# Chunked inputs of the clipped scan, and later stores of parts with interleaved maxima in three 16-head attentions

## The chip, the cores and the metric

The kernel runs on one core of one Trainium2 chip, as one program. The metric is the device time of one execution in microseconds (us); a result is the median of several executions. Engines: PE is TensorE (PEld its weight loads), DVE is VectorE, ACT is ScalarE, POOL is GpSimd, SP is SyncE. "ACTq" and "SPq" are the sequencers of ACT and SP issuing DMAs.

## The reference

A network of four layers works on X of 2048 tokens by 128. Each layer adds to X, in turn, a mixer, a feed-forward part and an attention (or the same in another order), twelve sublayers in all. The change touches four of them. Three are attentions of 16 heads of size 8:

```python
q, k, v = (heads(Wq, bq), heads(Wk, bk), heads(Wv, bv))
cos, sin = _rope_cos_sin(T, D)
q = _apply_rope(q, cos, sin)
k = _apply_rope(k, cos, sin)
att = jnp.einsum('bhqd,bhkd->bhqk', q, k) * (1.0 / np.sqrt(D))
att = jnp.where(causal[None, None], att, NEG_BIG)
att = jax.nn.softmax(att, axis=-1)
y = jnp.einsum('bhqk,bhkd->bhqd', att, v)
```

That is L0b, causal and rotary. L2b is the same without rotation and mask, and L3b has q and k filtered over the tokens instead; these two are called plain here. The fourth sublayer, L1a, is a scan with clipped states:

```python
xc = jax.lax.conv_general_dilated(xc, conv_w, window_strides=(1,), padding=[(K - 1, 0)], ...)
xi = _silu(jnp.transpose(xc, (0, 2, 1)))
dt_low = jnp.einsum('bld,rd->blr', xi, x_proj_w)
delta = jax.nn.softplus(jnp.einsum('blr,dr->bld', dt_low, dt_proj_w) + dt_proj_b)
delta = jnp.clip(delta, 1e-06, 10.0)
A = jnp.clip(-jnp.exp(A_log), -10.0, -1e-06)
e = jnp.clip(jnp.exp(delta * A), 1e-06, 1.0)
```

after which state = clip(state * e + xi) runs over the tokens. Here 256 channels are two halves of 128, and K is 4 taps.

## The kernel before, in words

The program is a sequence of stages. Each stage is one or a few blocks, and all engines meet at a block's end: none starts the next block before the slowest has issued its last instruction of this one. X, its normed copy nT and other activations lie in SBUF as [128, 2048] in fp32; a chunk is 512 tokens (CW), NC = 4 chunks.

**Attention, preparation** (`prepare_heads`). q and k are each split into three bf16 parts (high, middle, low), made by DVE (L777) and ACT (L791); DVE doubles two of the q parts (L781). A head's scores come from one matmul with 123 rows: products of parts, stacked, and rows that subtract the maxima. For that the parts of head 0 are copied by SP (L717, L722) straight into the row tiles qs[0], ks[0]; for all other heads the parts are stored by ACT's queue in DRAM (`store_part`, `store_twice`: eight DMAs of 512 KB, L725, L726, L729), from where SP loads each head's rows. ACT issues the stores last, after its copies of v (L794).

**Attention, heads** (`head_loop`). For each head the maxima of the scores per query are computed first: a "unit" is one tile of 128 queries by up to 1024 keys, two matmuls with 48 rows (L994) into one of two PSUM tiles (mps), in the causal case with the mask added by another matmul (L1000) on the diagonal, then one reduction by DVE (L1133). There are U = 24 units a head when causal, 32 when plain. When a head's units are reduced, DVE joins them (L1119), POOL splits them into three bf16 parts (L427 to L431), PE turns them (L1008, `turn_max`), ACT copies them (L1086), and a DMA puts them into row 72 and following of qs (L1096 by ACT for head 0, L946 by SP for the others). Only then can the head's scores start (L1018, S = 40 tiles when causal, 64 when plain), three PSUM tiles (SB), each with an exponential on ACT (L1105), then the products with v (L1039, L1042) into `ops`, which ACT copies out once a head (L1092) at its exponential n = OUT of the next head.

PE's stream is fixed: before head 0's scores it issues U + 3 units, `turn_max(0)` and 5 units more (U + AHEAD). After that, behind score n of head h, it issues units until `due(h, n)` are done, so that the next head's units run under this head's scores, two at a time (BURST). `turn_max(h + 1)` stands after score TURN = S - 7. In the causal case a pair of units signals DVE together (`ins.then_inc(mx_ready, len(xs))`). DVE joins head h - 1 after its first reduction of head h. SP in `head_loop` waits for the stores, then loads the rows of head 1, the missing half of head 0, the small products, and two heads ahead from there on.

In the trace these are stages 5, 8 and 9 (L0b: rows, preparation, heads), 36, 38, 39 (L2b) and 59, 63, 64 (L3b).

**Scan, inputs and decays** (`causal_scan_layer`, stages 13 to 18). After the input projection five blocks follow: the taps on DVE over all 2048 tokens (L1292, L1294) with silu on ACT (L1301); two projections (L361, 8 matmuls each) with copies by ACT and DVE; `softplus` (L1356 to L1368) with Exp and Ln in turn on ACT; and the decays (L1312 to L1329). Then `clipped_scan` begins (L1393).

## Time and profile before

| | |
|---|---|
| median of 3 runs | 5204.46 us (5199.28, 5204.46, 5205.0) |
| profiled execution | 5199.7 us, span 5197.9 us |
| busy: PE, DVE, ACT, POOL | 86%, 62%, 51%, 19% |
| mean granted clock of PE | 0.918 |
| causal attention's heads | from 364.3 us to about 910 us |
| plain attentions' heads | from 2461.5 us and from 4183.8 us |
| scan's inputs and decays | 1228.2 to 1292.3 us |

The granted clock is the share of 2.4 GHz that TensorE got, so 0.50 is 1.2 GHz. A row of the timeline gives the start, the busy time of a run of like instructions, the engine, the line, the operation, and in brackets how long the engine idled before and what released it.

### The profile page before, as it was taken

The page shows a single profiled execution, that of the slowest core. Times are in us where ns is not written, and L with a number is a line of the kernel's source. Part 1 is how long each engine was busy: PE and PEld are TensorE (multiplying, and loading weights), DVE is VectorE, ACT ScalarE, POOL GpSimd, SP SyncE. Part 2 cuts the span into 40 slices and gives each one's busy share as a digit, 9 for nine tenths or more (in the row PEclk, how much of TensorE's full clock was granted, in tenths as well). Part 3 has the DMA queues.
Part 4 walks back from the last instruction along what each step waited for, and adds up shares of the span by engine and source line. Part 5 has one row for each costly group of instructions (what it writes and reads, how often), then busy time and mean ns, then how long its engine had stood idle before and what let it go on. Part 6 is the DMA issues. An engine that isn't in the chain of part 4 may idle for free. (4 is left out here: it accounts for less than half of the span.)

```text
span 5197.9 us, 65865 instructions
## 1 busy us (share of the span) xinstructions
PE 4488.1 (86%) x22389; PEld 1663.4 (32%) x22441; DVE 3223.0 (62%) x4634; ACT 2648.4 (51%) x4913; POOL 976.2 (19%) x920
## 2 busy tenths in 40 slices
PE   6978888795189999867999997688869889999899
PEld 3432222442033333243122223355544412222244
DVE  4366664435865555254988883437963488888433
ACT  2325666334224444433588885344433348888633
POOL 0000000000038777800000000047940000000000
PEclk8979999897599999978899998898979979999999
DMA  1011110000000000001100000110000010000000
GB/s 62 20 67 35 35 35 20 17 16 0 7 1 3 5 3 5 5 28 37 36 28 28 27 18 2 56 62 3 1 9 16 11 68 26 26 26 26 3 21 20
DMA packets 44620, 118.99 MB, mean 23 GB/s; under 512 B 14463, under 2 KB 15863, under 8 KB 43287
## 3 DMA queue, kind: packets, MB, share of 16 engines
q1 hardware_dynamic: 37235, 98.19, 5.7%
q10 hardware_dynamic: 4524, 15.78, 0.8%
q8 instruction: 166, 2.72, 0.2%
q0 software_dynamic: 2560, 1.19, 0.1%
q14 instruction: 135, 1.11, 0.1%
HBM read 87.89 MB, written 19.01 MB: 21 GB/s over the span
## 5 line engine op out<-in xcount | busy, mean ns | idle before, releaser
L1133 DVE TENSOR_REDUCE 64_heads_mx<-64_heads_mps 128x1 f32<-128x1024 f32 x512 | 604.1, 1220 | 64.3 <-PE 64_heads_mps L994 63.1
L1133 DVE TENSOR_REDUCE 39_heads_mx<-39_heads_mps 128x1 f32<-128x1024 f32 x512 | 604.1, 1220 | 64.3 <-PE 39_heads_mps L994 63.2
L1105 ACT ACTIVATE 64_heads_p<-64_heads_sps 128x512 f32<-128x512 f32 x1024 | 552.8, 596 | 111.2 <-PE 64_heads_sps L1018 107.3
L1105 ACT ACTIVATE 39_heads_p<-39_heads_sps 128x512 f32<-128x512 f32 x1024 | 552.7, 596 | 111.3 <-PE 39_heads_sps L1018 107.3
L2106 ACT ACTIVATE 27_latent_heads_p<-27_latent_heads_ring 128x512 f32<-128x512 f32 x512 | 277.3, 595 | 385.4 <-PE 27_latent_heads_ring L2025 374.1
L1133 DVE TENSOR_REDUCE 9_heads_mx<-9_heads_mps 128x1 f32<-128x1024 f32 (+7 forms) x384 | 334.2, 908 | 179.7 <-PE 9_heads_mps L1000 173.3
L2124 DVE TENSOR_REDUCE 27_latent_heads_mx<-27_latent_heads_ring 128x1 f32<-128x512 f32 x512 | 323.1, 684 | 197.4 <-PE 27_latent_heads_ring L2005 197.4
L1105 ACT ACTIVATE 9_heads_p<-9_heads_sps 128x512 f32<-128x512 f32 (+3 forms) x640 | 304.3, 535 | 190.0 <-PE 9_heads_sps L1021 161.6
L1018 PE MATMUL 64_heads_sps<-59_head_rows_qs,59_head_rows_ks 123*128 123x512 bf16 x1024 | 311.3, 386 | 4.9 <-ACT 64_heads_p L1105 4.9
L1018 PE MATMUL 39_heads_sps<-36_head_rows_qs,36_head_rows_ks 123*128 123x512 bf16 x1024 | 310.9, 385 | 5.2 <-ACT 39_heads_p L1105 5.2
L1981 POOL TENSOR_TENSOR 27_latent_heads_psum<-27_latent_heads_psum,27_latent_heads_p 128x1024 f32<-128x1024 f32 x112 | 263.1, 2349 | 87.8 <-ACT 27_latent_heads_p L2106 87.8
L2021 PE MATMUL 27_latent_heads_ring<-27_latent_heads_qc,23_mla_mem_keys 64*128 64x512 f32 x1024 | 272.7, 609 | 3.4 <-DMA 24_mla_loop_mem_mrow<-27_latent_heads_mT 3.4
L1042 PE MATMUL 39_heads_ops<-39_heads_p,L2b_v 128*9 128x512 f32 x2048 | 267.8, 595 | 0.2 <-ACT 39_heads_osb L1092 0.2
L1042 PE MATMUL 64_heads_ops<-64_heads_p,L3b_v 128*9 128x512 f32 x2048 | 267.8, 595 | 0.2 <-ACT 64_heads_osb L1092 0.2
L1976 POOL TENSOR_TENSOR 27_latent_heads_psum<-27_latent_heads_psum,27_latent_heads_p 128x1024 f32<-128x1024 f32 x112 | 263.3, 2351 | 23.0 <-ACT 27_latent_heads_p L2106 23.0
L2005 PE MATMUL 27_latent_heads_ring<-23_mla_mem_keys,27_latent_heads_qc 64*128 64x512 f32 x1024 | 265.1, 609 | 1.9 <-DVE 27_latent_heads_mx L2124 0.5
L994 PE MATMUL 64_heads_mps<-59_head_rows_ks,59_head_rows_qs 48*128 48x512 bf16 x1024 | 187.6, 403 | 23.3 <-PEq L755 15.3
L994 PE MATMUL 39_heads_mps<-36_head_rows_ks,36_head_rows_qs 48*128 48x512 bf16 x1024 | 187.7, 403 | 18.1 <-PEq L755 10.0
L1018 PE MATMUL 9_heads_sps<-5_head_rows_qs,5_head_rows_ks 123*128 123x512 bf16 (+3 forms) x640 | 183.4, 353 | 11.5 <-ACT 9_heads_p L1105 4.3
L427 POOL CAST 64_heads_mparts<-64_heads_m 128x16 bf16<-128x16 f32 x16 | 3.1, 196 | 973.9 <-DVE 64_heads_m L1119 973.9
L615 DVE TENSOR_TENSOR 4_experts_hg<-4_experts_hr,4_experts_gps 128x512 f32<-128x512 f32 x128 | 88.0, 687 | 147.8 <-ACT 4_experts_hr L602 147.5
L615 DVE TENSOR_TENSOR 67_experts_hg<-67_experts_hr,67_experts_gps 128x512 f32<-128x512 f32 x128 | 88.0, 688 | 146.4 <-ACT 67_experts_hr L602 146.1
(1119 smaller groups left out, 7456.7 us busy)
## 6 DMA issues: line engine op xcount, KB each, us to landing
44_hale_masks_qs<-scratch_q_parts SPq DMA_DIRECT2D x45, 96.0 KB
44_hale_masks_ks<-scratch_k_parts SPq DMA_DIRECT2D x45, 96.0 KB
4_experts_wbuf<-in_L0f_experts SPq DMA_DIRECT2D x8, 514.0 KB, 3.5
12_experts_wbuf<-in_L0f_experts SPq DMA_DIRECT2D x8, 514.0 KB, 3.4
58_experts_wbuf<-in_L3f_experts SPq DMA_DIRECT2D x8, 514.0 KB, 3.5
67_experts_wbuf<-in_L3f_experts SPq DMA_DIRECT2D x8, 514.0 KB, 3.5
5_head_rows_qs<-scratch_q_parts SPq DMA_DIRECT2D x47, 64.0 KB
5_head_rows_ks<-scratch_k_parts SPq DMA_DIRECT2D x47, 64.0 KB
```

The costliest lines, as they stand in the source:

```text
L615: dve.tensor_tensor(hg[n % SLOTS][:], hr[n % SLOTS][:], gps[n // NF % 2][:], ALU.mult).then_inc(hg_ready, 1)
L994: ins = pe.matmul(mps[x % 2][:, b:b + n], qs[h % SETS][low:low + SIX, tile(i)], ks[h % SETS][low:low + SIX, 1024 * half + b:1024 * half + ...
L1018: ins = pe.matmul(sps[e % SB][:, 0:CW - off], ks[h % SETS][0:SUM_ROWS, tile(j)], qs[h % SETS][0:SUM_ROWS, c * CW + off:(c + 1) * CW], star ...
L1042: ins = pe.matmul(ops[row:row + ROW, off:CW], Vt[:, j, h, :], p, start=(s == 0), stop=(causal or s == NG - 1), tile_position=(0, row), ski ...
L1105: act.activation(pslot[x % PS][:, 0:CW - off], sps[e % SB][:, 0:CW - off], ACT.Exp, scale=SCALE / 2).then_inc(ex_done, 1)
L1133: dve.tensor_reduce(mx[h % 2][:, i, half:half + 1], mps[x % 2][:, 0:w], AX.X, ALU.max).then_inc(mx_taken, 1)
L1976: pool.tensor_tensor(psum[:, 0, :], so_far, slot(p, h)[:], ALU.add).then_inc(added_even, 1)
L1981: pool.tensor_tensor(psum[:, 1, :], so_far, slot(p, h)[:], ALU.add).then_inc(added_odd, 1)
L2005: pe.matmul(bank(number, x)[:], qc[h % 2][half, tile(i)], keys[half, chunk(2 * (u % 2) + x)], start=True, stop=True).then_inc(mx_ready, 1)
L2021: pe.matmul(bank(number, x)[:], keys[half, tile(j)], qc[h % 2][half, chunk(2 * (p % 2) + x)], start=True, stop=False)
L2106: act.activation(slot(p, h)[:, x * CW:(x + 1) * CW], bank(score_number(p, h), x)[:], ACT.Exp, scale=MLA_SCALE).then_inc(ex_done, 1)
L2124: dve.tensor_reduce(mx[:, w // NC, w % NC:w % NC + 1], bank(max_number(w // 2, h), w % 2)[:], AX.X, ALU.max).then_inc(mx_taken, 1)
```

## The change

1. `HeadRows.store` gathers the eight stores. In the three attentions (those with `doubled`) ACT issues them no longer at the end of `prepare_heads` but at the start of its stream in `head_loop`, once head 0's copies have landed. A fourth user of `prepare_heads`, a local attention, keeps them in place.
2. SP loads the rows of head 1 behind head 0's second half and small products.
3. `FIRST` and `WAIT` replace part of AHEAD for head 0: causal, 24 units and `turn_max(0)` stand before the scores, and the units of head 1 are issued behind scores 8 to 27; plain, 34 units, `turn_max(0)`, 2 units. DVE joins head 0 before its first reduction of head 1.
4. Each unit signals DVE by itself, a diagonal one after its own mask.
5. OUT is 4 in the causal case.
6. The scan's inputs and decays become one block, `causal_inputs`, by chunks: the first tap on ACT, three on DVE, silu, both projections and their copies chunk by chunk; then all eight Exp, all eight Ln, all eight decays.

```diff
                 eng.dma_start(self.ks[0][DH * i:DH * (i + 1), :], self.k[a][0:DH, :]).then_inc(self.rows_in[0], 16)

-    def store_part(self, g, eng, a):
-        eng.dma_start(g.scratch["q_parts"][a], self.q[a][:]).then_inc(self.stored, 16)
-        eng.dma_start(g.scratch["k_parts"][a], self.k[a][:]).then_inc(self.stored, 16)
-
-    def store_twice(self, g, eng, n):
-        eng.dma_start(g.scratch["q_parts"][3 + n], self.twice[n][:]).then_inc(self.stored, 16)
+    def store(self, g, eng):
+        for a in range(3):
+            eng.dma_start(g.scratch["q_parts"][a], self.q[a][:]).then_inc(self.stored, 16)
+            eng.dma_start(g.scratch["k_parts"][a], self.k[a][:]).then_inc(self.stored, 16)
+        for a, t in enumerate(self.twice):
+            eng.dma_start(g.scratch["q_parts"][3 + a], t[:]).then_inc(self.stored, 16)

...
                                    ACT.Identity).then_inc(v_done, 1)
-                for a in range(3):
+                if not doubled:
                     for s in "qk":
-                        wait_for_part(act, s, a)
-                    rows.store_part(g, act, a)
-                for n in range(len(twice)):
-                    act.wait_ge(two_done, n + 1)
-                    rows.store_twice(g, act, n)
+                        for a in range(3):
+                            wait_for_part(act, s, a)
+                    rows.store(g, act)
...
+    FIRST, WAIT = (0, 8) if causal else (4, 0)
     TURN = S - 7
     LATE = 4 if causal else 6
     BURST = 2
-    OUT = 6
+    OUT = 4 if causal else 6
     A = P // HEADS
     N = HEADS * S
     qs, ks, rows_in = rows.qs, rows.ks, rows.rows_in
...
         def due(h, n):
-            return min(HEADS * U, U + AHEAD + h * U + (n + 1) * U // (S * BURST) * BURST)
+            steady = min(HEADS * U, U + AHEAD + h * U + (n + 1) * U // (S * BURST) * BURST)
+            if h:
+                return steady
+            begun = max(0, n + 1 - WAIT)
+            return min(steady, U + FIRST + begun * (U - FIRST) // ((TURN - 5 - WAIT) * BURST) * BURST)

...
-        assert U + AHEAD + (TURN - 4) * U // S >= 2 * U
+        assert due(0, TURN) >= 2 * U
...
                 sp.wait_ge(rows.filled, rows.FILLED)
                 sp.wait_ge(rows.stored, rows.STORED)
-                load_rows(sp, 1)
                 for a in range(3):
                     load_queries(g, sp, 0, a, qs[0], m_in[0], (1,))
                     load_keys(g, sp, 0, a, ks[0], m_in[0], (1,))
                 load_products(sp, 0)
+                load_rows(sp, 1)
                 load_products(sp, 1)
                 sp.dma_start(spread[:], g.big["head_spread"].rearrange("p (a q) -> p a q", q=P)).then_inc(spread_in, 16)
...
+                        if not diag:
+                            ins.then_inc(mx_ready, 1)
                     for x in xs:
                         _i, _half, w, diag = units[x % U]
                         if diag:
-                            ins = pe.matmul(mps[x % 2][:, w - P:w], g.ident_bf[:], g.mask_q[:], start=False, stop=True)
-                    ins.then_inc(mx_ready, len(xs))
+                            pe.matmul(mps[x % 2][:, w - P:w], g.ident_bf[:], g.mask_q[:], start=False, stop=True).then_inc(mx_ready, 1)

                 def turn_max(h):
                     e = turned(h)
...
-                while x < U + 3:
+                while x < U + FIRST // 2:
                     max_pass([x])
                     x += 1
                 turn_max(0)
-                while x < U + AHEAD:
+                while x < U + FIRST:
                     max_pass([x])
                     x += 1
                 late = []
...
+                act.wait_ge(rows_in[0], SIX_COPIED)
+                rows.store(g, act)
                 copy_max(0)
                 act.wait_ge(ex_done, 1)
                 act.dma_start(qs[0][TWICE:SUM_ROWS, :], mT[0][:]).then_inc(m_in[0], 16)
...
+                    if u == 0 and h == 1:
+                        join_max(0)
                     dve.wait_ge(mx_ready, x + 1)
                     dve.tensor_reduce(mx[h % 2][:, i, half:half + 1], mps[x % 2][:, 0:w], AX.X, ALU.max).then_inc(mx_taken, 1)
-                    if u == 0 and h:
+                    if u == 0 and h >= 2:
                         join_max(h - 1)
                 join_max(HEADS - 1)
                 for i in range(2):
...
-            dt_low = inner.sb("dt_low", [64, T])
...
-            project(g, "dt_low", [Job(dt_low, [(W["L1a_xproj"][:, 0:64], u[0]), (W["L1a_xproj"][:, 64:128], u[1])])], ready)
-            project(g, "dt", [Job(acc[i], [(W["L1a_dtproj"][:, i * P:(i + 1) * P], dt_low)], W["L1a_dtb"][:, i:i + 1])
-                              for i in range(2)], ready)
-            softplus(g, acc, xi)
...
+            causal_inputs(g, xi, acc, u, e)
         states = [g.nT, g.yT]
...
+def causal_inputs(g, xi, acc, u, e):
...
+        low_ps = [st.ps(f"low{i}", [P, CW]) for i in range(2)]
+        dt_ps = [st.ps(f"dt{i}", [P, CW]) for i in range(6)]
...
+                low_rank(0)
+                for c in range(1, NC):
+                    low_rank(c)
+                    step_sizes(c - 1)
+                step_sizes(NC - 1)
...
+                act.wait_ge(padded, 2)
+                tap(0)
+                tap(1)
+                silu(0)
+                copy_low(0)
+                tap(2)
+                silu(1)
+                copy_low(1)
+                copy_sizes(0)
+                tap(3)
+                silu(2)
+                copy_low(2)
+                copy_sizes(1)
+                silu(3)
+                copy_low(3)
+                copy_sizes(2)
+                copy_sizes(3)
+                act.activation(A[:], W["L1a_Alog"], ACT.Exp).then_inc(A_exp, 1)
+                for n, (c, i) in enumerate(steps):
+                    act.wait_ge(size_ready, n + 1)
+                    act.activation(xi[i][:, chunk(c)], xi[i][:, chunk(c)], ACT.Exp, scale=-1.0).then_inc(tail_exp, 1)
+                for n, (c, i) in enumerate(steps):
+                    act.wait_ge(tail_exp, n + 1)
+                    act.activation(xi[i][:, chunk(c)], xi[i][:, chunk(c)], ACT.Ln, bias=1.0).then_inc(tail_ln, 1)
+                act.wait_ge(A_done, 2)
+                for n, (c, i) in enumerate(steps):
+                    act.wait_ge(bounded, n + 1)
+                    act.activation(flat[i][:, chunk(c)], acc[i][:, chunk(c)], ACT.Exp, scale=A[:, i:i + 1]).then_inc(decayed, 1)
+
+                def other_taps(c):
+                    for k in range(1, K):
+                        for i in range(2):
+                            if k == 1:
+                                dve.wait_ge(first_tap, 2 * c + i + 1)
+                            else:
+                                dve.wait_ge(taps, 2 * (K - 1) * c + 2 * (k - 2) + i + 1)
+                            dve.scalar_tensor_tensor(acc[i][:, chunk(c)], xi[i][:, c * CW + k:(c + 1) * CW + k],
+                                                     W["L1a_conv"][:, i * K + k:i * K + k + 1], acc[i][:, chunk(c)],
+                                                     ALU.mult, ALU.add).then_inc(taps, 1)
...
+                other_taps(0)
+                other_taps(1)
+                other_taps(2)
+                other_taps(3)
+                for c in range(NC):
+                    size(c)
...
+                for n, (c, i) in enumerate(steps):
+                    dve.wait_ge(tail_ln, n + 1)
+                    dve.scalar_tensor_tensor(acc[i][:, chunk(c)], acc[i][:, chunk(c)], 0.0, xi[i][:, chunk(c)], ALU.max, ALU.add).then_inc(summed, 1)
+                    if n:
+                        bound(n - 1)
+                bound(NS - 1)
+                for n, (c, i) in enumerate(steps):
+                    dve.wait_ge(decayed, n + 1)
+                    dve.tensor_scalar(flat[i][:, chunk(c)], flat[i][:, chunk(c)], 1e-6, 1.0, ALU.max, ALU.min).then_inc(e_done, 1)
```

ACT's stream at the end of the preparation in L0b (9_heads_mT is head 0's maxima), the change as a difference:

```order
-L725 DMA scratch_q_parts<-5_head_rows_q 128x2048
-L726 DMA scratch_k_parts<-5_head_rows_k 128x2048
-L725 DMA scratch_q_parts<-5_head_rows_q 128x2048
-L726 DMA scratch_k_parts<-5_head_rows_k 128x2048
-L725 DMA scratch_q_parts<-5_head_rows_q 128x2048
-L726 DMA scratch_k_parts<-5_head_rows_k 128x2048
+L755 UNCONDITIONAL_BRANCH
+L1085 UNCONDITIONAL_BRANCH
+L726 DMA scratch_q_parts<-5_head_rows_q 128x2048
+L727 DMA scratch_k_parts<-5_head_rows_k 128x2048
```

The block ends at the branches. The stores stood ahead of them and now stand behind.

PE's stream in L0b around the turn of head 0's maxima (L1008, now L1014), before:

```order
L994 MATMUL 9_heads_mps<-5_head_rows_ks,5_head_rows_qs 128x512 x2
L1008 MATMUL 9_heads_sps<-ident_bf,9_heads_mparts 48x128
L994 MATMUL 9_heads_mps<-5_head_rows_ks,5_head_rows_qs 128x128
L1000 MATMUL 9_heads_mps<-mask_q_bf,ident_bf 128x128
L994 MATMUL 9_heads_mps<-5_head_rows_ks,5_head_rows_qs 128x512 x2
L994 MATMUL 9_heads_mps<-5_head_rows_ks,5_head_rows_qs 128x256
L1000 MATMUL 9_heads_mps<-mask_q_bf,ident_bf 128x128
L994 MATMUL 9_heads_mps<-5_head_rows_ks,5_head_rows_qs 128x512 x2
L994 MATMUL 9_heads_mps<-5_head_rows_ks,5_head_rows_qs 128x256
L1000 MATMUL 9_heads_mps<-mask_q_bf,ident_bf 128x128
L1018 MATMUL 9_heads_sps<-5_head_rows_qs,5_head_rows_ks 128x512
```

and after:

```order
L1014 MATMUL 9_heads_sps<-ident_bf,9_heads_mparts 48x128
L1024 MATMUL 9_heads_sps<-5_head_rows_qs,5_head_rows_ks 128x512
L1027 MATMUL 9_heads_sps<-mask_k_bf,ident_bf 128x128
L1024 MATMUL 9_heads_sps<-5_head_rows_qs,5_head_rows_ks 128x512 x3
L1024 MATMUL 9_heads_sps<-5_head_rows_qs,5_head_rows_ks 128x384
L1027 MATMUL 9_heads_sps<-mask_k_bf,ident_bf 128x128
L1024 MATMUL 9_heads_sps<-5_head_rows_qs,5_head_rows_ks 128x512 x3
L1045 MATMUL 9_heads_ops<-9_heads_p,9_heads_Vz 25x512 x4
```

No unit stands between the turn and the first scores any more.

The same place in L2b (stage 39, now 37; two L994, now L999, are one unit), before:

```order
L994 MATMUL 39_heads_mps<-36_head_rows_ks,36_head_rows_qs 128x512 x70
L1008 MATMUL 39_heads_sps<-ident_bf,39_heads_mparts 48x128
L994 MATMUL 39_heads_mps<-36_head_rows_ks,36_head_rows_qs 128x512 x10
L1018 MATMUL 39_heads_sps<-36_head_rows_qs,36_head_rows_ks 128x512 x4
L994 MATMUL 39_heads_mps<-36_head_rows_ks,36_head_rows_qs 128x512 x4
```

and after:

```order
L999 MATMUL 37_heads_mps<-34_head_rows_ks,34_head_rows_qs 128x512 x68
L1014 MATMUL 37_heads_sps<-ident_bf,37_heads_mparts 48x128
L999 MATMUL 37_heads_mps<-34_head_rows_ks,34_head_rows_qs 128x512 x4
L1024 MATMUL 37_heads_sps<-34_head_rows_qs,34_head_rows_ks 128x512 x4
L999 MATMUL 37_heads_mps<-34_head_rows_ks,34_head_rows_qs 128x512 x4
```

Forty units ahead of the first score become 36. Further on, in head 0, the 65th and 66th unit stand behind score 52 before and behind score 56 now, while the turn of head 1's maxima stands behind score 58 in both.

## Rows read from the trace of the kernel before

**Rows 1.** Timeline, causal attention, where the preparation ends and the heads start.

```profile
357.49 0.62 ACT L794 ACTIVATE L0b_v<-8_prepare_vps 128x512 f32<-128x512 f32 x1
...
361.46 2.39 ACTq L729 DMA_DIRECT2D scratch_q_parts<-5_head_rows_twice  x2
...
364.32 1.12 PE L994 MATMUL 9_heads_mps<-5_head_rows_ks,5_head_rows_qs 48*128 48x512 bf16 x3 [8.31 <-PEq L755]
```

**Rows 2.** Timeline, the same place in the first plain attention.

```profile
2455.26 0.61 ACT L794 ACTIVATE L2b_v<-38_prepare_vps 128x512 f32<-128x512 f32 x1
...
2461.51 1.44 PE L994 MATMUL 39_heads_mps<-36_head_rows_ks,36_head_rows_qs 48*128 48x512 bf16 x3 [9.97 <-PEq L755]
```

**Rows 3.** Timeline, causal attention, from head 0's last maxima to its first scores.

```profile
393.64 1.22 DVE L1133 TENSOR_REDUCE 9_heads_mx<-9_heads_mps 128x1 f32<-128x1024 f32 x1
...
394.77 0.17 DVE L1119 TENSOR_REDUCE 9_heads_m<-9_heads_mx 128x16 f32<-128x32 f32 x1
...
397.02 1.38 ACTq L1096 DMA_DIRECT2D 5_head_rows_qs<-9_heads_mT  x1
...
404.07 0.61 PE L1018 MATMUL 9_heads_sps<-5_head_rows_qs,5_head_rows_ks 123*128 123x512 bf16 x1 [4.04 <-DMA 5_head_rows_qs<-9_heads_mT]
```

**Rows 4.** Timeline, the same chain in the first plain attention.

```profile
2501.30 0.17 DVE L1119 TENSOR_REDUCE 39_heads_m<-39_heads_mx 128x16 f32<-128x32 f32 x1
...
2503.54 0.80 ACTq L1096 DMA_DIRECT2D 36_head_rows_qs<-39_heads_mT  x1
...
2507.87 1.03 PE L1018 MATMUL 39_heads_sps<-36_head_rows_qs,36_head_rows_ks 123*128 123x512 bf16 x2
```

**Rows 5.** Timeline, plain attention, the turn of head 1's maxima in head 0.

```profile
2541.26 0.60 PE L994 MATMUL 39_heads_mps<-36_head_rows_ks,36_head_rows_qs 48*128 48x512 bf16 x4
...
2543.85 0.81 PE L994 MATMUL 39_heads_mps<-36_head_rows_ks,36_head_rows_qs 48*128 48x512 bf16 x4
...
2544.32 0.20 POOL L431 CAST 39_heads_mparts<-39_heads_mrest 128x16 bf16<-128x16 f32 x1
...
2545.12 0.24 PE L1008 MATMUL 39_heads_sps<-ident_bf,39_heads_mparts 128*48 128x128 bf16 x1
```

**Rows 6.** Waits of PE, 433 to 878 us (total us, times, longest).

```profile
PE 9_heads_mps L994 <- DVE 9_heads_mx L1133: 24.2, 42, 0.8
PE 9_heads_ops L1039 <- ACT 9_heads_osb L1092: 11.8, 14, 0.8
```

**Rows 7.** Page, costliest groups (xcount | busy, mean ns | idle before, releaser).

```profile
L1133 DVE TENSOR_REDUCE 9_heads_mx<-9_heads_mps 128x1 f32<-128x1024 f32 (+7 forms) x384 | 334.2, 908 | 179.7 <-PE 9_heads_mps L1000 173.3
```

**Rows 8.** Tile 9_heads_mT, the queue's line (ns min/median/max, first and last start).

```profile
L946 SPq DMA_DIRECT2D 5_head_rows_qs<-9_heads_mT x15: 733/734/753, 431.2 to 882.0; - x15
```

**Rows 9.** Tile 9_heads_p, the last head of the causal attention.

```profile
L1105 ACT ACTIVATE 9_heads_p<-9_heads_sps x40: 277/592/632, 885.8 to 907.8; 128x512 f32<-128x512 f32 x28, 128x384 f32<-128x384 f32 x4, 128x256 f32<-128x256 f32 x4, 128x128 f32<-128x128 f32 x4
```

**Rows 10.** Timeline of the scan's inputs and decays.

```profile
1228.16 1.29 DVE L1292 TENSOR_SCALAR 14_in_acc<-14_in_xi,weights_L1a 128x2048 f32<-128x2048 f32 x1
1229.49 7.13 DVE L1294 SCALAR_TENSOR_TENSOR 14_in_acc<-14_in_xi,weights_L1a,14_in_acc 128x2048 f32<-128x2048 f32 x3
...
1247.44 9.14 PE L361 MATMUL 16_dt_low_bank<-13_mamba_mem_u,weights_L1a 128*64 128x512 f32 x16 [20.47 <-PEq L1283]
...
1257.62 7.10 PE L361 MATMUL 17_dt_bank<-14_in_dt_low,weights_L1a 64*128 64x512 f32 x16 [1.04 <-PEq L351]
...
1265.80 1.28 ACT L1366 ACT_TABLE_LOAD   x1 [1.21 <-PEq L351]
...
1292.31 3.69 ACT L1393 ACTIVATE 19_clipped_e_turned<-13_mamba_mem_e 128x2048 f32<-128x2048 f32 x1 [1.85 <-PEq L1309]
```

**Rows 11.** Groups by form on DVE: a tap of 512 tokens in another layer.

```profile
L1570 DVE SCALAR_TENSOR_TENSOR 30_ssm_mem_acc<-30_ssm_mem_xi,weights_L2a,30_ssm_mem_acc 128x512 f32<-128x512 f32 x16 | 10.8, 738 | 0.9 <-ACT 30_ssm_mem_acc L1518 0.9
```

**Rows 12.** Windows: us, busy of PE, PEld, DVE, ACT, POOL, granted clock, DMA, GB/s.

```profile
404.00:406.00 2.00, 1.93 (x5) 0.49 (x5) 0.00 (x0) 1.18 (x3) 0.00 (x0) 0.50 0.13 51
408.00:410.00 2.00, 1.90 (x11) 0.46 (x13) 1.41 (x3) 1.44 (x4) 0.00 (x0) 0.86 0.00 0
```

126 lines of the change are left out of this document (66 added, 60 removed).

## Prediction, made before the changed kernel ran

> **What bounds the kernel now.** I read the page's busy shares first: TensorE 86%, no other engine above 62%. So a saving counts only where PE waits, and there at full size. Then I read the timeline at the places that the diff touches, and PE's waits in the steady part of the causal attention.
>
> Where the preparation ends and the heads start, the reader is to see who came last. In L0b ACT's last copy of v ends at 358.11, the last store leaves ACT's queue at 363.85, and PE starts 0.47 us later, after 8.31 us idle [rows 1]. So the block was held by ACT issuing stores. In L2b the gap between the copy's end, 2455.87, and PE's start, 2461.51, is 5.6 us [rows 2]. L3b is like L2b.
>
> From head 0's join on DVE to its first score there are 9.3 us in L0b (394.77 to 404.07), and the last thing waited for is the DMA of the turned maxima [rows 3]. In L2b it is 6.6 us and PE does not wait for the DMA; it is busy with passes until then [rows 4]. In the steady part of the causal loop PE's two largest waits come to 36.0 us in 14 heads, 2.6 us a head [rows 6]; a head takes (882.0 - 431.2)/14 = 32.2 us [rows 8]. The scan's inputs take 64.15 us, 1228.16 to 1292.31 [rows 10], in which PE works 16 us: DVE, ACT and PE take turns.
>
> **1. Stores behind the block.** PE would start 0.47 us after ACT's last copy: 358.58 instead of 364.32, -5.7 [rows 1], and 2456.34 instead of 2461.51, -5.2 in each plain attention [rows 2]. Together **-16.1**. The eight stores still have to be made: they cost some 7 us of ACT's queue, while ACT has nothing to do until head 0's maxima are turned, over 35 us later [rows 1, 3]. SP's loads of rows come later against PE by that much; head 0's second half and its products now stand ahead of head 1's rows, and both are wanted only about 35 us after the start. If that cover were gone, PE would wait up to the 7 us once in each attention.
>
> **2. Head 0's chain.** Causal: DVE joins before the first reduction of head 1 and not after it, which saves that reduction, 1.22 us [rows 3]: **-1.2**. Plain: the join would come at 2501.30 - 1.2 = 2500.1. With the 9.3 us of [rows 3] the first score comes at 2509.4, not 2507.87: +1.5 each. I take L0b's chain since the loads of head 1 and 2 run beside it there as they would here; a quicker DMA is rival D.
>
> **3. Head 1's units under head 0, causal.** Twenty-four units stand behind scores 8 to 27 instead of 16 spread from the start, 8 of them done ahead. The first 8 exponentials without units take (907.8 - 885.8)/39 = 0.56 us each, 4.5 [rows 9]. The dense stretch is DVE's: at 334.2/384 = 0.87 busy each [rows 7] it is 21 us at least; PE and DVE hand two PSUM tiles to and fro, and with some 0.17 between reductions it is 25; at 1.2 us a unit, the pace of the stretch before the scores, 29. The last 12 go at 32.2/40 = 0.8, 9.7. Sum 39.2 against 32.2: **+7.0**, ends +3 and +11. The 8 units that left the stretch ahead of the scores give nothing there, since PE waited for the DMA anyway.
>
> **4. Plain.** Four units more lie inside the loop, where PE is the bound: four L994, two units, take 0.81 [rows 5], so +1.6. And the join of head 1 needs the 65th unit, issued behind score 52 before and 56 now, while the turn stays behind score 58. From that unit's pass at 2541.26 to POOL's last split, 2544.52, is 3.26 us [rows 5]; two scores with their share of all else cover 1.3 of it. PE would stand for the other **1.95**, with everything queued behind the turn: products, scores, passes. With 1.5 from step 2 that is 5.05 each, **+10.1** for both. Below nothing it can't be, except by D; at most it is +14.
>
> **5. The causal loop.** OUT = 4 lets ACT copy out two exponentials earlier; the wait of PE for it was 11.8/14 = 0.84 a head. Signals by unit let DVE start a pair's first reduction while PE does the second; of 24.2/14 = 1.73 I take 0.5. 1.3 by 15 heads: **-19**. Ends: -8, if half of the first is all, and -28, if both waits go nearly wholly [rows 6].
>
> **6. Scan inputs.** Phase one, chunk by chunk: ACT has two taps, two silus and three copies, seven of about 0.68, 4.8 us; it also waits in order for the low-rank product, two matmuls of 7.10/8 = 0.89 [rows 10], and for hand-overs of about 0.9. That is 7.5 a chunk, 30. DVE's 24 taps at 10.8/16 = 0.675 [rows 11] are 16 us and hide in it. TensorE comes out of 20 us of idleness: the first eight matmuls took 9.14, the later ones 7.10. I let the first chunk run at 1.2 GHz: 4 matmuls by 0.89 more, 34. Phase two: eight Exp, eight Ln, eight Exp of 0.62 (a copy of the same size [rows 1]) with a table load of 1.28 ahead of each set, 18.7, and 1.5 at the ends: 20.2. With 0.5 to the scan's first copy, 54.7 against 64.2: **-9.5**. Ends: -13.4 with the clock full throughout, +0.5 if all 16 matmuls run at half.
>
> For the taps a row and a rule differ. Three 2048-wide taps took 7.13 us [rows 10], 0.594 for 512 tokens; a 512-wide one takes 0.675 [rows 11]. 
>
> **Rivals.**
>
> **A**, the forecast: 0.62.
>
> **B. The next wait takes the loop's gain** (0.12). PE's largest wait is for DVE's reductions, in 42 places [rows 6]. DVE needs 24 by 0.87 = 21 of a head's 32.2 us, which speaks against; that PE would only wait at the next of the 24 speaks for it. Then -19 is about nothing: 5193, called 5192.
>
> **C. Half clock in the new blocks** (0.08). The matmuls in the scan block are sparse, and the dense stretch of head 0 takes its upper end: 10 of one or some of both, about 5184.
>
> **D. The DMA of the maxima is quick** (0.08). In L0b it took 7 us from 397.02 to the score [rows 3] with head 2's loads on SP's queue; in L2b it took at most 4.3 [rows 4]. If it takes 4.3 in all three, the chain is 2.7 shorter in each, and what later SP loads cost disappears: -8 to -11, 5163. This hangs on how the loads of another queue hold up a small transfer. The Trainium skill, DMA: Bandwidth & Descriptors, section on queues, rings and completion order, says that each DMA engine takes packets of the queues in turn, so a small transfer on ACT's queue would not wait behind SP's whole backlog. By that rule D is right; L0b's 7 us [rows 3] speaks against.
>
> **E. TensorE stays at 1.2 GHz through head 0: slower** (0.04). The granted clock was 0.50 at 404 to 406, after the wait for the maxima, and 0.86 at 408 to 410 [rows 12]. Now PE idles through the whole chain, and scores come alone at first. PE is busy some 29 of a causal head's 32.2 us [rows 6, 8], so one head at half clock costs 29, in a plain attention more. One such head cancels the gain (-28.7 + 29); two make the kernel slower, about 5232. It decides from the second attention on. That the clock rose within 6 us in the old order speaks against.
>
> **F. Something else holds the block** (0.06): SP's last copies or DVE's doublings end just behind ACT's last store. DVE's and SP's last work stands ahead of 357 in L0b, so I doubt it. It would cost step 1: 5190.
>
> **How the numbers follow.** A single run of this kernel can't tell less than 0.2%, about 10.4 us, from no change, so faster means under 5194. Of A that is 0.61, of B 0.08, of C 0.07, D 0.08, of F 0.03: **0.87**. The rest of these is the same, **0.09**; E, with more than one head at half clock, is slower, **0.04**. The range, **5158 to 5192**: downwards the ends of steps 5, 6 and 2 (-9, -4, -3) joined in part, upwards to B and F. Beyond lie E, B's worse half and a sum at all its good ends.
>
> **What would show each step.** The first L999 (once L994) about 0.5 us after the last L794, with L726 to L729 behind it. First score of head 0 at 9 us behind its join in all three. Head 0's exponentials of L0b spanning 39 us before head 1's. In L2b and L3b one wait of PE for POOL's split of 2 us in head 0. PE's wait for osb gone in the causal loop and a head of 30.9 us. The scan's inputs in 55 us. Wrong would be: a head period unchanged at 32.2; loads of head 1 that PE waits for; a granted clock of 0.50 more than a few us into head 0.

## The result and the profile after

The changed kernel takes 5187.81 us (median of 6 runs, 5183.81 to 5191.73) against 5204.73 for the kernel before in the same comparison (6 runs). The ratio is 0.9966, 95% interval 0.9956 to 0.9976: 17 to 18 us faster, where 28.7 had been worked out and 5174 named. The time lies inside the range. The profiled execution took 5190.05 us, span 5188.3. That is 9.6 less than the profiled one of before; the table below shows where the rest of the 17 went.

The page of the changed kernel, busy time by engine (us, share of the span, instructions):

```profile
span 5188.3 us, 65875 instructions
PE 4512.1 (87%) x22389; PEld 1669.7 (32%) x22441; DVE 3216.1 (62%) x4666; ACT 2656.8 (51%) x4949; POOL 976.0 (19%) x920
```

PE has the same 22389 instructions and is busy 24 us longer, which is a first hint that some of them ran at the lower clock. The spans of both profiled executions, worked out from starts and ends in the timelines (a head lasts from its first exponential to the next head's; the scan's part starts with its first MEMSET, 0.2 us ahead of the first tap from which [rows 10] counts 64.15; "forecast" is the prediction's):

| us | before | after | difference | forecast |
|---|---|---|---|---|
| causal: start of the heads, from the last copy's end | 6.2 | 0.3 | -5.9 | -5.7 |
| causal: start to first exponential | 40.5 | 39.0 | -1.5 | -1.2 |
| causal: head 0 | 31.9 | 41.4 | +9.5 | +7.0 |
| causal: heads 1 to 15 to the last exponential | 471.7 | 446.2 | -25.5 | -19 |
| scan's inputs and decays | 64.4 | 56.8 | -7.6 | -9.5 |
| L2b and L3b: start of the heads, from the last copy's end | 5.6, 5.7 | 0.5, 0.5 | -5.1, -5.2 | -5.2 each |
| L2b and L3b: start to first exponential | 47.0, 47.0 | 48.3, 48.8 | +1.3, +1.8 | +1.5 each |
| L2b and L3b: head 0 | 41.9, 41.9 | 49.2, 48.8 | +7.3, +6.9 | +3.55 each |
| L2b and L3b: head 1 | 42.1, 42.1 | 44.5, 46.0 | +2.4, +3.9 | 0 |
| local attention (unchanged steps) | 175.6 | 183.9 | +8.3 | 0 |

Without the last row the sum is -17.7; the medians differ by 16.9 and the ratio gives 17.7. The local attention, with the changed kernel's code, took 176.3 to 192.3 us in the profiles of ten kernels below. With the stores ordered as before it took 175.6 us in the kernel before, and 181.8 and 183.0 in two kernels below. So it varies that much from one profile to another, and no effect of the change on it is shown.

The start of the heads in L0b, timeline of the changed kernel, which answers to [rows 1]:

```profile
356.47 2.06 ACT L794 ACTIVATE L0b_v<-8_prepare_vps 128x512 f32<-128x512 f32 x4 [1.59 <-PE 8_prepare_vps L763]
...
358.82 0.36 ACTq L726 DMA_DIRECT2D scratch_q_parts<-5_head_rows_q  x1
358.84 0.65 PE L999 MATMUL 9_heads_mps<-5_head_rows_ks,5_head_rows_qs 48*128 48x512 bf16 x3 [2.41 <-PEq L755]
```

PE starts 0.3 us after ACT's last copy, at the same moment as the first store. In L2b the copies end at 2424.43 and PE starts at 2424.93.

The chain to head 0's first score in L0b, which answers to [rows 3], and the same in L2b, which answers to [rows 4]:

```profile
387.79 0.19 DVE L1128 TENSOR_REDUCE 9_heads_m<-9_heads_mx 128x16 f32<-128x32 f32 x1
...
390.04 1.63 ACTq L1105 DMA_DIRECT2D 5_head_rows_qs<-9_heads_mT  x1
...
397.08 0.61 PE L1024 MATMUL 9_heads_sps<-5_head_rows_qs,5_head_rows_ks 123*128 123x512 bf16 x1 [7.38 <-DMA 5_head_rows_qs<-9_heads_mT]
```

```profile
2463.28 0.19 DVE L1128 TENSOR_REDUCE 37_heads_m<-37_heads_mx 128x16 f32<-128x32 f32 x1
...
2465.53 0.81 ACTq L1105 DMA_DIRECT2D 34_head_rows_qs<-37_heads_mT  x1
...
2472.59 1.46 PE L1024 MATMUL 37_heads_sps<-34_head_rows_qs,34_head_rows_ks 123*128 123x512 bf16 x3 [6.20 <-DMA 34_head_rows_qs<-37_heads_mT]
```

It is 9.3 us each, from the join to the score, and PE now waits for the DMA in both. So the 9.3 of [rows 3] carried over.

The waits of PE in the steady causal loop of the changed kernel, which answer to [rows 6], and the queue's line of tile 9_heads_mT, which answers to [rows 8]:

```profile
PE 9_heads_mps L999 <- DVE 9_heads_mx L1144: 21.1, 44, 0.8
PE 9_heads_sps L1024 <- ACT 9_heads_p L1114: 3.6, 14, 0.3
PE 9_heads_sps L1014 <- POOL 9_heads_mparts L431: 0.3, 1, 0.3
```

```profile
L951 SPq DMA_DIRECT2D 5_head_rows_qs<-9_heads_mT x15: 732/734/747, 434.0 to 860.1; - x15
```

PE's wait for ACT's copy, 11.8 us before, is gone, and so is its wait for POOL's split, 6.2 us. The wait for DVE only fell from 24.2 to 21.1. The head takes 30.49 us instead of 32.29.

Head 0 of L0b holds something that the forecast had only among its rivals. Near the end of its dense stretch of units PE waits for DVE unit by unit, up to 0.83 us at a time, and the clock falls right behind these waits (columns as in [rows 12]):

```profile
423.00:426.00 3.00, 1.43 (x10) 0.49 (x10) 2.36 (x3) 0.84 (x2) 0.00 (x0) 1.00 0.00 0
427.00:430.00 3.00, 3.00 (x15) 0.55 (x13) 1.96 (x2) 0.18 (x1) 0.00 (x0) 0.50 0.00 0
```

Now the place in L2b that cost most, head 0's turn of head 1's maxima, which answers to [rows 5]; then the end of head 0:

```profile
2515.71 0.30 PE L1014 MATMUL 37_heads_sps<-ident_bf,37_heads_mparts 128*48 128x128 bf16 x1 [2.17 <-POOL 37_heads_mparts L431]
2515.94 1.90 PE L1048 MATMUL 37_heads_ops<-37_heads_p,L2b_v 128*9 128x512 f32 x8
...
2517.77 1.03 PE L1024 MATMUL 37_heads_sps<-34_head_rows_qs,34_head_rows_ks 123*128 123x512 bf16 x2
...
2523.14 0.39 PE L999 MATMUL 37_heads_mps<-34_head_rows_ks,34_head_rows_qs 48*128 48x512 bf16 x2 [0.75 <-DVE 37_heads_mx L1144]
2524.27 0.39 PE L999 MATMUL 37_heads_mps<-34_head_rows_ks,34_head_rows_qs 48*128 48x512 bf16 x2 [0.74 <-DVE 37_heads_mx L1144]
...
2525.01 0.60 ACT L1114 ACTIVATE 37_heads_p<-37_heads_sps 128x512 f32<-128x512 f32 x1 [1.99 <-PE 37_heads_sps L1024]
```

and the windows of the changed kernel around the turn (columns as in [rows 12]):

```profile
2513.00:2516.00 3.00, 0.83 (x9) 0.22 (x11) 2.35 (x3) 1.45 (x3) 1.02 (x5) 0.93 0.00 0
2516.00:2518.00 2.00, 2.00 (x10) 0.20 (x10) 0.00 (x0) 0.27 (x1) 0.00 (x0) 0.50 0.03 6
```

PE stood for 2.17 us, close to the 1.95 of the forecast. Then the granted clock was 0.50 for some 3 us, and eight product matmuls took 1.90 us where the same eight take 1.05 elsewhere in this head. Seven us on, as units 69 to 72 come close together, PE waits twice 0.75 us for DVE, and ACT idles 1.99.

The scan block of the changed kernel, which answers to [rows 10]:

```profile
1205.34 0.09 DVE L1431 MEMSET 14_in_xi<- 128x3 f32 x2 [1.96 <-PEq L139]
...
1214.87 0.59 ACT L1368 ACTIVATE 16_causal_in_low<-16_causal_in_low 64x512 f32<-64x512 f32 x1 [3.77 <-PE 16_causal_in_low L1334]
...
1224.82 4.06 DVE L1416 SCALAR_TENSOR_TENSOR 14_in_acc<-14_in_xi,weights_L1a,14_in_acc 128x512 f32<-128x512 f32 x6 [4.65 <-ACT 14_in_acc L1357]
...
1226.68 3.67 PE L1334 MATMUL 16_causal_in_low<-13_mamba_mem_u,weights_L1a 128*64 128x512 f32 x4 [3.22 <-ACT 13_mamba_mem_u L1363]
1230.29 3.78 PE L1344 MATMUL 16_causal_in_dt<-16_causal_in_low,weights_L1a 64*128 64x512 f32 x4
...
1243.79 1.28 ACT L1395 ACT_TABLE_LOAD   x1
...
1262.11 3.69 ACT L1476 ACTIVATE 17_clipped_e_turned<-13_mamba_mem_e 128x2048 f32<-128x2048 f32 x1 [0.76 <-PEq L1326]
```

The first phase ends with the table load at 1243.79, 38.4 us after the start, where 34 was forecast; the second takes 18.3 to the scan's first copy, where 20.7 was. Two matmuls (four instructions in the trace) take 3.67 to 3.78 us, 1.8 to 1.9 each, twice the 0.89 of [rows 10]. The granted clock was 0.68 on average from 1211 to 1244 us, so nearly two thirds of that stretch ran at 1.2 GHz. ACT waits for them (3.77) and DVE, behind ACT's first taps, waits 4.65.

### The profile page after: what moved, and what is told of

The parts are those of the page before. It is cut to its first block and busy times, and to the rows that moved or that the text cites. A ratio compares the mean times of both kernels' runs of the same rounds, so it can differ in the third digit from the quotient of the medians.

```text
span 5188.3 us, 65875 instructions
## 1 busy us (share of the span) xinstructions
PE 4512.1 (87%) x22389; PEld 1669.7 (32%) x22441; DVE 3216.1 (62%) x4666; ACT 2656.8 (51%) x4949; POOL 976.0 (19%) x920
## 5 line engine op out<-in xcount | busy, mean ns | idle before, releaser
L1144 DVE TENSOR_REDUCE 62_heads_mx<-62_heads_mps 128x1 f32<-128x1024 f32 x512 | 603.6, 1219 | 77.2 <-PE 62_heads_mps L999 76.1
L1144 DVE TENSOR_REDUCE 37_heads_mx<-37_heads_mps 128x1 f32<-128x1024 f32 x512 | 603.6, 1219 | 75.5 <-PE 37_heads_mps L999 74.4
L1114 ACT ACTIVATE 62_heads_p<-62_heads_sps 128x512 f32<-128x512 f32 x1024 | 552.5, 596 | 123.1 <-PE 62_heads_sps L1024 119.6
L1114 ACT ACTIVATE 37_heads_p<-37_heads_sps 128x512 f32<-128x512 f32 x1024 | 552.4, 596 | 122.0 <-PE 37_heads_sps L1024 118.5
L2189 ACT ACTIVATE 25_latent_heads_p<-25_latent_heads_ring 128x512 f32<-128x512 f32 x512 | 277.3, 594 | 385.4 <-PE 25_latent_heads_ring L2108 374.1
L2207 DVE TENSOR_REDUCE 25_latent_heads_mx<-25_latent_heads_ring 128x1 f32<-128x512 f32 x512 | 322.9, 684 | 197.7 <-PE 25_latent_heads_ring L2088 197.7
L1024 PE MATMUL 62_heads_sps<-57_head_rows_qs,57_head_rows_ks 123*128 123x512 bf16 x1024 | 312.7, 388 | 12.0 <-DMA 57_head_rows_qs<-62_heads_mT 6.3
L1024 PE MATMUL 37_heads_sps<-34_head_rows_qs,34_head_rows_ks 123*128 123x512 bf16 x1024 | 311.9, 387 | 11.9 <-DMA 34_head_rows_qs<-37_heads_mT 6.2
L2064 POOL TENSOR_TENSOR 25_latent_heads_psum<-25_latent_heads_psum,25_latent_heads_p 128x1024 f32<-128x1024 f32 x112 | 263.5, 2353 | 87.8 <-ACT 25_latent_heads_p L2189 87.8
L2104 PE MATMUL 25_latent_heads_ring<-25_latent_heads_qc,21_mla_mem_keys 64*128 64x512 f32 x1024 | 272.8, 609 | 3.4 <-DMA 22_mla_loop_mem_mrow<-25_latent_heads_mT 3.4
L2059 POOL TENSOR_TENSOR 25_latent_heads_psum<-25_latent_heads_psum,25_latent_heads_p 128x1024 f32<-128x1024 f32 x112 | 263.6, 2354 | 23.1 <-ACT 25_latent_heads_p L2189 23.1
L999 PE MATMUL 62_heads_mps<-57_head_rows_ks,57_head_rows_qs 48*128 48x512 bf16 x1024 | 187.2, 402 | 18.6 <-DMA 57_head_rows_ks<-57_head_rows_k 10.1
L999 PE MATMUL 37_heads_mps<-34_head_rows_ks,34_head_rows_qs 48*128 48x512 bf16 x1024 | 186.3, 401 | 12.2 <-DVE 37_heads_mx L1144 7.1
```

The source lines that it names most:

```text
L999: ins = pe.matmul(mps[x % 2][:, b:b + n], qs[h % SETS][low:low + SIX, tile(i)], ks[h % SETS][low:low + SIX, 1024 * half + b:1024 * half + ...
L1024: ins = pe.matmul(sps[e % SB][:, 0:CW - off], ks[h % SETS][0:SUM_ROWS, tile(j)], qs[h % SETS][0:SUM_ROWS, c * CW + off:(c + 1) * CW], star ...
L1114: act.activation(pslot[x % PS][:, 0:CW - off], sps[e % SB][:, 0:CW - off], ACT.Exp, scale=SCALE / 2).then_inc(ex_done, 1)
L1144: dve.tensor_reduce(mx[h % 2][:, i, half:half + 1], mps[x % 2][:, 0:w], AX.X, ALU.max).then_inc(mx_taken, 1)
L2059: pool.tensor_tensor(psum[:, 0, :], so_far, slot(p, h)[:], ALU.add).then_inc(added_even, 1)
L2064: pool.tensor_tensor(psum[:, 1, :], so_far, slot(p, h)[:], ALU.add).then_inc(added_odd, 1)
```

## The experiments

The theory after the result: what the change lost are the units of head 1 that it moved behind head 0's scores. The rivals: the later loads of rows, and the clock. Each run states its ratio to the kernel before on the same chip; the changed kernel's is 0.9966.

**Eight units ahead in the plain attentions.**

```diff
-    FIRST, WAIT = (0, 8) if causal else (4, 0)
+    FIRST, WAIT = (0, 8) if causal else (8, 0)
-            if h:
+            if h or not causal:
                 return steady
```

> Edit: in the two plain attentions eight units of head 1 stand ahead of head 0's first score and the rate behind the scores is the steady one, as before; all else as changed. Theory (the units moved behind the scores are what the plain attentions lost): head 0 of L2b falls from 49.2 us to about 42 and head 1 from 44.4 to 42.1, PE's wait for POOL's split in head 0 (2.2 us) goes, and the first score comes at about the same time, so each plain attention is 9 to 10 us shorter and the kernel 17 to 20 us faster than the changed one, about 5169. Rival (the later loads of rows, behind the later stores, hold head 0 and head 1): heads 0 and 1 stay at 49 and 44 us and the time stays near 5188.

Measured: 5167.71 us, ratio 0.9936 (0.9922 to 0.9949), 15.6 us under the changed kernel's ratio. Head 0 took 41.9 us in both attentions and head 1 42.1; the whole heads part 718.4 against 726.6 and 728.3. The first exponential came 49.7 us after the start in both, 1.4 and 0.9 us later. From the first score, for which PE waited 3.1 us, to beyond the turn of head 1 in L2b, no other wait of PE is left: the split's 2.2 us is gone. The theory holds and the rival falls, since the loads were the same. The gain is a little less than the 17 to 20 us expected.

**Eight units ahead in the causal attention.** The same edit with `(8, 0) if causal else (4, 0)`.

> Edit: in the causal attention eight units of head 1 stand ahead of head 0's first score and the steady rate behind, as before; all else as changed. Theory: head 0 falls from 41.4 us to about 30.5, since the dense stretch of 24 units in 19 scores is DVE's bound; the first score comes 0 to 2 us later, since PE waited 6 us for the maxima there anyway; the kernel is 8 to 11 us faster than the changed one, about 5178. Rival (head 0 is held by the loads or the clock, not by units): head 0 stays above 38 us and the time near 5188.

Measured: 5184.36 us, ratio 0.9964 (0.9951 to 0.9978), no gain that can be told. Head 0 fell to 30.9 us as expected, but the first exponential moved from 39.0 to 46.0 us after the start. The timeline of this run shows why:

```profile
392.76 0.71 PE L999 MATMUL 9_heads_mps<-5_head_rows_ks,5_head_rows_qs 48*128 48x512 bf16 x3 [6.28 <-DMA 5_head_rows_ks<-scratch_k_parts]
...
403.52 0.61 PE L1024 MATMUL 9_heads_sps<-5_head_rows_qs,5_head_rows_ks 123*128 123x512 bf16 x1 [3.92 <-DMA 5_head_rows_qs<-9_heads_mT]
```

PE reached head 1's first unit and stood 6.28 us for head 1's rows, with the turn of head 0's maxima behind it in its stream. So the dense stretch in the changed kernel pays for something: with late stores and head 1's rows last, those rows aren't there earlier. In this run the scan block also took 61.5 us and not 56.8, its matmuls all at 0.50 of the clock from 1220 on; that is rival C of the prediction, seen by chance. It makes the profiled execution (5188.48 us, the slowest of the five) about 5 us longer; whether the other four had it isn't known. The run shows one more thing, in L3b, whose code is the changed kernel's. At the turn of head 1's maxima PE stood for 2.17 us, up to 4253.02, as in the changed kernel, but the clock did not fall behind it:

```profile
4253.00:4262.00 9.00, 7.49 (x47) 1.60 (x47) 6.62 (x6) 4.71 (x9) 0.00 (x0) 1.00 0.07 22
```

Head 0 took 47.45 us there instead of 48.81.

**The scan as before.** The five blocks restored.

> Edit: the scan's inputs and decays in the five blocks of before; the attentions as changed. Theory: it gives back 7.6 us, the difference of the two profiles over this part: about 5195.5. Rival (chunks gain nothing of their own and the difference is the state of the clock): within 3 us of 5188.

Measured: 5192.87 us, ratio 0.9983 (0.9974 to 0.9993), 8.8 us over the changed kernel, where 7.6 were expected. The block took 64.3 us again.

**The stores as before.**

```diff
-                act.wait_ge(rows_in[0], SIX_COPIED)
-                rows.store(g, act)
```

with `store_part` and `store_twice` at the end of the preparation again.

> Edit: ACT issues the stores at the end of the preparation again, in all four users; all else as changed. Theory: each of the three attentions starts 5.2 to 5.7 us later and nothing is won back in head 0: 14 to 17 us slower than the changed kernel, about 5204. Rival (the late stores delay the loads of rows and cost in heads 0 and 1 what the early start wins): head 0 of the plain attentions shorter than 49 us and the time within 5 us of 5188. The local attention, whose stores the change made wait for all parts, took 8.2 us longer in the changed kernel's profile; if its order of stores is the cause, that part is 8 us shorter here, if it is chance it is not.

Measured: 5195.67 us, ratio 0.9984 (0.9975 to 0.9993), 9.4 us over the changed kernel, where 14 to 17 were expected. By the profile it is 11.3: the three starts are 16.8 us later, one of the heads' parts is 0.4 us longer, the other two 2.1 and 3.8 shorter. So the truth lies between theory and rival. What the late stores give back isn't in heads 0 and 1 (49.3 and 44.4 us in L2b here too) but ahead of them. From the issue of the maxima's transfer to the first score there are 4.4 and 3.9 us in the plain attentions here, and 7.1 and 7.2 in the changed kernel. The local attention took 181.8 us here: its order of stores is not what lengthened it.

**The turn first.** FIRST is 4 when causal and 8 when plain. The rate behind the scores is the steady one when plain; when causal it is the changed kernel's, without its pause of 8 scores. And

```diff
-                while x < U + FIRST // 2:
+                while x < U:
                     max_pass([x])
```

> Edit on the changed kernel: the turn of head 0's maxima stands right behind head 0's units; behind it 4 units of head 1 in the causal attention (rate up to the turn as the changed kernel's formula gives it, without its pause) and 8 in the plain ones (steady rate, as before). Theory (PE in its fixed order waits for head 1's rows before the turn, which delayed the first score by 7.0 us in the run with eight ahead, and the dense stretch costs head 0): causal first score 39 to 41 us after PE's start, head 0 at 31 to 34 us, heads part 7 to 9 us shorter than the changed kernel's 526.7; plain first exponential 48 to 49 us after the start, heads 0 and 1 at 42, 717 us in all; the kernel at 5155 to 5162. Rival (head 1's rows arrive so late that they hold the units ahead of the first score wherever the turn stands): causal first score at 44 us or later, kernel above 5165.

Measured: 5163.63 us, ratio 0.9922 (0.9909 to 0.9936). Causal: first exponential at 39.0, head 0 34.0, heads part 519.3. Plain: 49.0 and 49.4, heads part 717.6 and 718.1. The places are as the theory had them; the time is 1.6 us above its range, and under the 5165 of the rival. PE still waits 4.2 us for head 1's rows, but with the turn already issued that wait lies under the transfer of the maxima.

**OUT = 6, and signals together.** Two runs, each with one part of the causal loop's change undone.

> Edit on the changed kernel: OUT = 6 in the causal attention too, as before. Theory (the wait of PE for ACT's copy of the products was 0.84 us a head): the causal period goes from 30.49 to about 31.3 us, kernel 11 to 13 us slower than the changed one, about 5200. Rival (all 1.8 us a head come from the signals by unit): the period stays at 30.5.

Measured: 5203.99 us, ratio 0.9996 (0.9987 to 1.0005), 15.6 us over the changed kernel, where 11 to 13 were expected. The period (from one causal head to the next) is 31.40 us and PE's wait for the copy is back at its old size:

```profile
PE 9_heads_ops L1045 <- ACT 9_heads_osb L1098: 11.8, 14, 0.8
```

> Edit on the changed kernel: the units of a causal pair signal DVE together again. Theory (the rest of the 1.8 us a head is from the signals): the period goes from 30.49 to about 31.4 us, kernel 13 to 16 us slower, about 5202. Rival (OUT gave it all): period 30.5. If both runs show more or less than their sum of 1.8, the two edits overlap.

Measured: 5207.01 us, ratio 1.0008 (0.9999 to 1.0017), 21.8 us over, where 13 to 16 were expected. The period is 31.37 us, and head 0 took 46.7 us instead of 41.4, which the expectation had left out. Its waits:

```profile
PE 9_heads_mps L999 <- DVE 9_heads_mx L1143: 24.2, 42, 0.8
PE 9_heads_sps L1013 <- POOL 9_heads_mparts L431: 6.3, 13, 0.5
```

So the 1.8 us a head are 0.9 from OUT and 0.9 from the signals; the two add up. The signals took away not only 3 us of the wait for DVE in 14 heads but the whole wait for the split at the turn, 6.3 us, since, by the order of DVE's stream, the join stands behind the first reduction of a pair, which now needn't wait for the second unit's matmuls.

**Eight ahead in the causal attention, head 1's rows first.**

```diff
                 sp.wait_ge(rows.stored, rows.STORED)
+                load_rows(sp, 1)
...
                 load_products(sp, 0)
-                load_rows(sp, 1)
```

> Edit on the run with eight units ahead in the causal attention: SP loads head 1's rows ahead of head 0's second half, as before. Theory (PE's 6.3 us of waiting for head 1's rows come from the later stores plus the new order of loads): the order is worth about half, the wait falls to 2 to 4 us, but the load of head 0's second half comes later and may be waited for at the first score, so the first exponential moves from 46.0 to 42 to 46 us; kernel 0 to 4 us faster than 5184. Rival (the order is all of it): the wait is gone and the first exponential is at 40.

Measured: 5176.47 us, ratio 0.9949 (0.9935 to 0.9963). PE's wait for head 1's rows is gone altogether, the first exponential is at 39.8, head 0 takes 30.7, the heads part 516.7. The rival was right: the order is all of the 6.3 us, not half, and head 0's second half is in time for the first score.

**Both together**: eight ahead and the steady rate everywhere, the turn behind two of the eight, head 1's rows first.

> Edit on the changed kernel, in all three attentions: eight units of head 1 ahead of head 0's first score, the steady rate behind (as before), the turn of head 0's maxima behind 2 of the eight, and SP loads head 1's rows first (as before). What stays of the change: later stores, signals by unit, OUT = 4, DVE's early join, the scan block. Theory (the units behind the scores and the order of loads are what the change lost): causal heads 515 to 517 us against 526.7, plain heads 717 us against 726.6 and 728.3, sum -28 to -31 against the changed kernel, about 5158. Rival (in the plain attentions head 1's rows first delay head 0's second half, wanted at the first score): plain first exponential above 50 us and the kernel above 5163.

Measured: 5158.84 us, ratio 0.9915 (0.9902 to 0.9929). Causal 516.4, plain 717.3 and 717.5. As expected.

**Head 2's rows held back** until head 0's maxima have landed (one wait on `m_in[0]` in SP's stream, on top of the last run).

> Edit on the run before it in this list: SP loads head 2's rows only when head 0's maxima have landed. Theory (the transfer of head 0's maxima takes 7.0 us instead of 4.0 to 4.4 where it shares the way with loads of rows): 4 us from issue to arrival, so PE's wait before the first causal score goes and the first exponential is 2 to 3 us earlier there; in the plain attentions the eight units hold it anyway, 0 to 1 us. Kernel 2 to 4 us faster than its neighbour. Rival (the 7 us are head 0's own second half, or the tail of the stores): no change, within 1 us in every attention.

Measured: 5150.65 us, ratio 0.9898 (0.9883 to 0.9914); the intervals of this run and its neighbour overlap, so the medians' 8 us are not all told from chance. In the profile the plain heads parts are 2.0 and 1.7 us shorter and the causal one is unchanged at 516.4. The expectation had it the other way round. The DMA packets of this run, while the maxima (12 KB) are on their way, say why; first L0b, 388.26 to 395.35 us, then L2b, 2455.47 to 2457.30 (queue, packets, MB, share of the 16 engines):

```profile
q1 hardware_dynamic: 109, 0.36, 12.5%
q10 hardware_dynamic: 51, 0.01, 0.8%
```

```profile
q10 hardware_dynamic: 51, 0.01, 3.0%
```

The 51 packets on q10 are the maxima, those on q1 SP's loads of rows. In L0b head 2's loads are held back, but the loads that SP had issued by 383.9 us, those of head 0's second half and of head 1, are still running, and the transfer takes 7.1 us as ever. In L2b nothing else moves: all 51 packets are done 1.8 us after the issue, and PE comes to the first score at 2460.93 from its units, without a wait.

**The stores early again**, on top of "both together".

> Edit on the first of this list: the stores at the end of the preparation again, as before. Theory (late stores let PE start 5.2 to 5.7 us earlier but give 2 to 3 back in a slower transfer of the maxima): 3 us an attention, 8 to 11 us slower than the first of this list. Rival (with the units in their old place all is given back): within 3 us.

Measured: 5172.25 us, ratio 0.9937 (0.9924 to 0.9951), 13.4 us over its neighbour, where 8 to 11 were expected. PE idles 8.31 us ahead of its start in L0b again. The causal heads part is 2.5 us longer (518.9), and the plain ones are 1.3 and 1.6 us shorter (716.0, 715.9). With the three starts 16.9 us later the profiles give 16.5 us for the later stores here and gave 11.3 beside the changed kernel's own order; the medians, 13.4 and 9.4, are not far enough apart to tell that from chance.

**All first taps first**, on top of "both together": ACT's order in the scan block is

```diff
                 tap(0)
                 tap(1)
+                tap(2)
+                tap(3)
                 silu(0)
+                silu(1)
                 copy_low(0)
-                tap(2)
-                silu(1)
+                silu(2)
                 copy_low(1)
                 copy_sizes(0)
-                tap(3)
-                silu(2)
+                silu(3)
...
```

> Edit on the first of this list: in the scan block ACT issues the first taps of all four chunks before anything else, and a chunk's silu before the copy of the chunk ahead. Theory (the first phase took 38.4 us and not 34 since ACT, in order, stands behind PE's matmuls at 1.2 GHz while DVE idles for its next tap): DVE's taps run without a gap, PE's matmuls stand closer; the phase falls to 30 to 36 us if the clock stays at 1.2 GHz and to 26 to 30 if it rises; kernel 3 to 11 us faster than the first of this list. Rival (PE's 16 matmuls at 1.8 us each are the bound): the phase at 37 us or more.

Measured: 5142.36 us, ratio 0.9883 (0.9868 to 0.9898), 16.5 us under its neighbour and, by the two ratios, 43 under the changed kernel: the fastest of all. The block takes 42.4 us instead of 56.8, the first phase 24.0 instead of 38.5. The timeline of PE and the windows of this run:

```profile
1199.74 5.47 PE L1334 MATMUL 16_causal_in_low<-13_mamba_mem_u,weights_L1a 128*64 128x512 f32 x8 [7.39 <-ACT 13_mamba_mem_u L1363]
1205.15 1.98 PE L1344 MATMUL 16_causal_in_dt<-16_causal_in_low,weights_L1a 64*128 64x512 f32 x4
1207.10 1.93 PE L1334 MATMUL 16_causal_in_low<-13_mamba_mem_u,weights_L1a 128*64 128x512 f32 x4
```

```profile
1199.00:1205.00 6.00, 5.25 (x8) 1.34 (x8) 6.00 (x11) 2.67 (x5) 0.00 (x0) 0.63 0.00 0
1205.00:1217.00 12.00, 11.50 (x25) 3.68 (x24) 9.62 (x15) 9.00 (x15) 0.00 (x0) 1.00 0.00 0
```

and the neighbour's windows, in its own block:

```profile
1201.00:1215.00 14.00, 10.08 (x12) 2.40 (x12) 8.02 (x12) 5.05 (x9) 0.00 (x0) 0.62 0.00 0
1215.00:1234.00 19.00, 13.51 (x21) 3.84 (x20) 8.41 (x13) 9.21 (x15) 0.00 (x0) 0.69 0.00 1
```

PE works nearly without a gap from 1199.74 on, its clock goes to 2.4 GHz and stays there, and the matmuls take half the time, which in turn releases ACT sooner. The gain is larger than the expectation's upper end of 11, and 14.4 of it are the block's in the profile. That the denser order raised the clock and the clock made the order denser still is how I read it; no run has the one without the other.

## Why the prediction was right, and where its sum was off

The direction, its size within a factor of two, and the range held. The range held partly by luck: the loop of step 5 gave 6.5 us more than its term and hid half of the 13.5 us by which step 4 was off. With step 5 at its -19 the time would have been about 5194, outside the range. By steps:

1. **Stores behind the block.** -16.1 forecast, -16.2 in the profile. But "the eight stores still have to be made" was costed at nothing where PE had other work: measured with the stores moved back, they give back 2.2 us in L2b ahead of the first score (48.3 against 46.1) and 3.2 in L3b, by a slower transfer of the maxima. The sum had 1.5 of each in step 2, by taking [rows 3] for the plain attentions.
2. **Head 0's chain.** -1.2 and +1.5 each; measured -1.5, +1.3 and +1.8.
3. **Head 1's units under head 0, causal.** +7.0, ends +3 and +11; measured +9.5, and head 0 is 10.5 shorter with eight ahead. Part of it is the clock, at 0.50 from 427 to 430 us behind PE's waits for DVE; in the run with eight ahead and head 1's rows first it was 1.00 from 402 to 430.
4. **Plain.** This is the step that failed: +10.1 for both, "at most it is +14"; measured +23.6 (+1.3, +7.3, +2.4 and +1.8, +6.9, +3.9 in the table). The stall of 1.95 at the turn was seen rightly, at 2.17. Three things were missing. First, the clock fell to 0.50 behind the stall, so score 60 came 3.7 and 3.6 us later against score 56 than before, and not 1.95. Seven of the profiled kernels have this turn twice, each time with the stall of 2.17. Behind 12 of the 14 the clock fell; behind two it stayed at 1.00, and there score 60 came 2.2 us later. One of the two is in L3b with eight ahead in the causal attention (its window stands with that run). So the stall cost 2.2 us and the clock another 1.3 to 1.4. Second, the four units inside the loop were priced as their matmuls' 1.6 us; up to score 56 they took 3.6 in L2b and 3.4 in L3b. In PE's order the units no longer stand between two scores and two scores, but beside three scores in a row, and four scores with their units took 2.92 us there instead of 2.6. That three PSUM tiles can't take three scores in a row without a wait is argued; no run shows it apart from the rest. Third, head 0's own rate ended 2 units behind the steady one, so four units came together at the head's end: PE's two waits and ACT's 1.99 us above, in no step of the forecast. L3b's head 1 lost 1.5 us more than L2b's, with the granted clock at 0.57 from 4263 to 4267 us.
5. **The causal loop.** -19, ends -8 and -28; measured -25.5, 1.8 a head by 13, and 1.0 each in the last two. OUT's 0.84 was right (0.9). The signals were taken at 0.5 from the wait for DVE alone; they gave 0.9, and two thirds of the waits that went were at the turn. The ends don't follow from [rows 6]: half of the first wait is 6 us in 15 heads, and both waits whole are 38.6, not 28.
6. **Scan inputs.** -9.5; measured -7.6. The second phase was 2.4 us shorter than forecast, the first 4.4 longer: the clock was taken at half for one chunk and was at half for nearly two thirds of the stretch with its matmuls.

Of the rivals, C came nearest in its mechanism, and with 5184 in its time. Both its terms, the sparse matmuls and the dense stretch, were off in the direction that it names, by 1.9 and 2.5 us; the 13.5 of step 4 were in no rival. B fell: the wait for DVE stayed at 21.1 us and took over nothing of the gain. D is right only where SP's queue runs empty early: in the plain attentions with the stores early, where the first score comes 4.4 or 3.9 us behind the issue, and with head 2's rows held back, where the packets take 1.8. In the causal attention it took 6.8 to 7.5 us in every run. The Trainium skill's rule that a DMA engine takes packets of its queues in turn (DMA: Bandwidth & Descriptors, on queues, rings and completion order) therefore does not by itself keep a small transfer quick: in the run that holds head 2's rows back its 51 packets were under way for 7 us beside 109 of SP's. E did not come: the causal attention's granted clock, 0.50 from 396 to 402 us, was 0.91 from 402 to 406, within 9 us of the first score at 397.08. F did not come: PE started 0.3 to 0.5 us behind the last copy in all three attentions.

The rule against small tiles (the Trainium skill, VectorE: DVE Perf Modes, on the TRN2 errata) did not decide either. DVE's six taps of a chunk took 4.06 us, 0.68 each, as in [rows 11]; by the rule's 58 cycles they would be 0.594, an estimate. The same section says of that row that it under-predicts and puts the measured fixed part at about 150 cycles, by which a tap would be 0.69, an estimate too, and the trace agrees with that one. Its advice is tiles of 512 elements or more, and the chunks have 512, so it did not speak against this change. What mattered was which engine stood behind which.

## What to carry to other kernels

Ahead of a first score that waits for a transfer, filler work is nearly free as long as its own data is there: four more units moved the first exponential by 0.9 to 1.4 us, and eight whose rows came late by 7. Behind the first score they cost more than their own time, and a rate that ends behind the steady one is paid again in a lump at the boundary. In an in-order engine's stream, put what starts a long chain (a turn, a first tap) ahead of what may wait for data. Look for gaps in a stage of sparse matmuls before making the stage smaller: here the clock fell behind a gap and was paid on top of it, 1.3 to 1.4 us behind one of 2.2.

## What the runs showed of the hardware

A pause of PE of 2.17 us in a stretch at a granted clock of 1.00 was followed by some 3 us at 0.50 in 12 of 14 cases, which cost 1.3 to 1.4 us on top of the pause; in the other two the clock stayed at 1.00. A row of shorter waits, none over 0.83 us, was followed by a clock of 0.50 too. Sixteen fp32 matmuls of 512 columns with gaps of 2 to 7 us between groups of two to six had a granted clock of 0.68 over 33 us, and in one run 0.50 from 1220 us to the end; the same sixteen without gaps reached 1.00 within some 5 us. A transfer of 12 KB from SBUF to SBUF was through in 1.8 us with nothing else under way, and came into use 3.9 to 7.5 us behind its issue where loads of rows ran beside it.
